# Attention and expert layer on one core: PE's turns placed between the score chunks, VectorE's remainders ahead of its maxima, row loop written out

## The reference, cut to what matters

```python
# x: (4, 2048, 256); 16 heads of 16
q, k, v = split(x @ Wqkv.T + bqkv);  q, k = rope(q), rope(k)
logits = einsum('bhid,bhjd->bhij', q, k) * SCALE
logits = einsum('bhij,gh->bgij', logits, Wpre)       # mix heads before softmax
attn = softmax(logits, axis=-1)
attn = einsum('bhij,gh->bgij', attn, Wpost)          # mix heads after softmax
out = einsum('bhij,bhjd->bhid', attn, v) -> (b, n, 256) @ Wout.T + bout
x = layernorm(x + out)
x = layernorm(x + soft_moe(x))                       # 16 experts, 16 slots
```

## Time and profile before

| | us |
|---|---|
| median of 3 runs | 9109.38 (9107.03 to 9111.76) |
| the profiled execution | 9096.98 |
| its span | 9094.8 |
| PE busy | 8336.7 (92%) |
| DVE busy | 7663.0 (84%) |
| ACT busy | 7243.9 (80%) |
| POOL busy | 5479.1 (60%) |

### The profile page before, as it was taken

The page is one execution under the profiler, slowest core; times in us unless marked ns, Lnnn a source line. Parts: engine busy times, 40 slices in busy tenths (PEclk is TensorE's granted clock), DMA queues, the critical chain, the costliest instruction groups (busy, mean ns, idle before and its releaser), DMA issues.

```text
span 9094.8 us, 401014 instructions
## 1 busy us (share of the span) xinstructions
PE 8336.7 (92%) x158060; PEld 4668.9 (51%) x158060; DVE 7663.0 (84%) x12269; ACT 7243.9 (80%) x13696; POOL 5479.1 (60%) x12005
## 2 busy tenths in 40 slices
PE   7999999997799999999779999999978999999997
PEld 4555555554455555555445555555544555555554
DVE  7888888886788888888678888888867888888886
ACT  5888888885588888888558888888856888888884
POOL 5666666663566666666356666666635666666663
PEclk9999999998899999999889999999988999999998
DMA  0000000002000000000200000000020000000002
GB/s 30 7 8 9 8 8 8 9 8 69 21 7 9 8 9 7 8 9 8 68 21 7 9 8 9 7 8 8 9 67 21 8 8 8 9 7 9 8 9 76
DMA packets 101046, 144.01 MB, mean 16 GB/s; under 512 B 8097, under 2 KB 90657, under 8 KB 96801
## 3 DMA queue, kind: packets, MB, share of 16 engines
q1 hardware_dynamic: 99104, 117.57, 3.9%
HBM read 75.60 MB, written 41.94 MB: 13 GB/s over the span
## 4 chain that ended last, share of the span: by engine, by line
PE 50%; DVE 23%; issue 15%; ACT 5%; POOL 3%; SPq 1%; DVEq 1%; DMA 1%; POOLq 1%; ACTq 0%
PE psS L1179 29%; PE psP L1199 11%; DVE top L821 7%; PE psO L1214 6%; DVE pl L861 5%; DVE big L835 5%; ACT big L648 3%; PE psM L1225 1%; ACT ph L658 1%; PE psS L1154 1%; PE psS L1311 1%; PE psS L1340 1%; ACT pr L630 1%; DVE rr L853 1%; PE psM L1239 1%
## 5 line engine op out<-in xcount | busy, mean ns | idle before, releaser
L835 DVE SCALAR_TENSOR_TENSOR big<-psP,big 128x512 f16<-128x512 f32 x4096 | 2628.1, 683 | 623.1 <-ACT big L648 610.6
L648 ACT ACTIVATE big<-psP 128x512 f16<-128x512 f32 x4096 | 2214.0, 592 | 1020.7 <-PE psO L1214 563.6
L821 DVE TENSOR_REDUCE top<-psS 128x1 f32<-128x1024 f32 x2048 | 2486.5, 1214 | 409.5 <-PE psS L1179 394.0
L1179 PE MATMUL psS<-KH,AH 128*128 128x512 f16 x8192 | 2471.9, 383 | 121.6 <-POOL AL L441 81.8
L1179 PE MATMUL psS<-KH,AL 128*128 128x512 f16 x8192 | 2448.5, 381 | 0.1
L1179 PE MATMUL psS<-KL,AH 128*128 128x512 f16 x8192 | 2446.3, 380 | 0.0
L630 ACT ACTIVATE pr<-psS,nb 128x1024 f32<-128x1024 f32 x2048 | 2281.7, 1114 | 67.9
L658 ACT ACTIVATE ph<-pr 128x1024 f16<-128x1024 f32 x2048 | 2151.2, 1050 | 32.4
L1199 PEld LDWEIGHTS psP<-rh,ph 64*128 64x128 f16 x32768 | 1434.7, 95 | 1093.1 <-issue 611.9
L861 DVE TENSOR_TENSOR pl<-pr,ph 128x1024 f16<-128x1024 f32 (+1 forms) x2048 | 1969.7, 962 | 0.6 <-ACT ph L658 0.4
L1199 PE MATMUL psP<-rh,ph 64*128 64x64 f16 x32768 | 1680.3, 192 | 213.4 <-POOL rl L535 175.0
(11 more groups left out here) (138 smaller groups left out, 7398.1 us busy)
## 6 DMA issues: line engine op xcount, KB each, us to landing
ph<-in_xT SPq DMA_DIRECT2D x16, 512.0 KB, 4.3
xr<-in_x SPq DMA_DIRECT2D x64, 128.0 KB, 2.4
d_x<-x SPq DMA_DIRECT2D x64, 128.0 KB, 1.7
d_xn<-xn SPq DMA_DIRECT2D x64, 128.0 KB, 1.7
d_lg<-lg SPq DMA_DIRECT2D x64, 128.0 KB, 1.7
d_ct<-cT SPq DMA_DIRECT2D x64, 128.0 KB, 1.7
Q<-in_w SPq DMA_DIRECT2D x8, 1024.0 KB, 12.4
out<-V SPq DMA_DIRECT2D x16, 512.0 KB, 3.3
```

The source lines that it names most:

```text
L648: a.activation(PT[:, hf * JH:(hf + 1) * JH, :, 0, i0:i0 + HQ], psP[:, ih, :].rearrange("p (j g i) -> p j g i", j=JH, g=H), ACT.Copy, scale ...
L821: v.tensor_reduce(top[:, t % 2, h:h + 1], psS[:, 2 * h:2 * h + 2, :].rearrange("p c n -> p (c n)"), X, ALU.max).then_inc(s_mx, 1)
L835: v.scalar_tensor_tensor(out=PT[:, js, :, 1, i0:i0 + HQ], in0=psP[:, ih, :].rearrange("p (j g i) -> p j g i", j=JH, g=H), scalar=MDROP, in ...
L1179: mm = pe.matmul(psS[:, c, :], A_[:, k8, k, :], K_[:, k, c * CW:(c + 1) * CW], start=n == 0, stop=n == 5)
```

## The change

PE places each turn between the two score chunks of a half (scores 0, turn 0, scores 1, scores 2, turn 1, scores 3). The four output pieces go to four places: piece 0 to the end of the slot before (t % 8 == 1), piece 1 behind scores 0, piece 2 behind scores 1, piece 3 behind scores 2 of t % 8 == 2. DVE runs the two `mixed_low` ahead of each `half_max`, `recip` behind `half_max` 0, and `low` 1 behind that. ACT runs `highs` of half 1 a slot later, between `mixed_high` 0, 1 and `bound` 0, and `highs` of half 0 behind `mixed_high` 2, 3. POOL runs `first_half`, `post` ahead of the tile preparation's high and low parts and its own `low` last. Row steps of PE, ACT and DVE move a slot earlier in several cases. The loop over the row groups is replaced by the groups written out.

```diff
-PE_SLOT = dict(y=3, turn_u=12, logits=13, turn_c=15)
-ACT_SLOT = dict(turn_u=12, weigh=14, turn_c=15)
+PE_SLOT = dict(y=3, turn_u=11, logits=12, turn_c=15)
+ACT_SLOT = dict(turn_u=11, weigh=13, turn_c=15)
 DVE_SLOT = dict(residual=4, stats=4, seed1=5, centre=6, norm1=8, norm2=8, squares=8, seed2=9,
-                keep=13, weigh=14, combine=15)
+                keep=12, weigh=13, combine=14)
...
# POOL
                     roots(t, work, 0)
                     if one:
-                        low(T - 1, t_1, first and t < 3)
+                        first_half(T - 1, t_1)
+                        post(T - 1, t_1)
                     if live:
                         mixq_high(it, t + LEAD)
+                    if one:
+                        post_high(T - 1, t_1, first and t < 5)
+                    if live:
+                        mixq_low(it, t + LEAD)
+                    if one:
+                        post_low(T - 1, t_1)
                     roots(t, work, 1)
                     if one:
-                        first_half(T - 1, t_1)
-                    if live:
-                        mixq_low(it, t + LEAD)
+                        low(T - 1, t_1, first and t < 3)
...
# ACT
                     mixed(0)
                     mixed(1)
+                    if not (first and t < 1) and (live or t < 1):
+                        highs(T - 1, (t - 1) % TI, 1, first and t < 3)
                     if live:
                         bound(T, t, 0)
                         exps(T, t, 0, early)
-                        highs(T, t, 0, early)
                     mixed(2)
                     mixed(3)
                     if live:
+                        highs(T, t, 0, early)
                         bound(T, t, 1)
                         exps(T, t, 1, early)
                         factor(T, t, early)
-                        highs(T, t, 1, early)
...
# DVE
+                    if two:
+                        mixed_low(T - 2, t_2, 0)
+                        mixed_low(T - 2, t_2, 1)
                     if live:
                         half_max(T, t, 0)
+                    if one:
+                        recip(T - 1, t_1)
                     rows(t, work, 0)
...
-                    if two:
-                        mixed_low(T - 2, t_2, 0)
-                        mixed_low(T - 2, t_2, 1)
-                    rows(t, work, 1)
                     if one:
                         low(T - 1, t_1, 1, first and t < 3)
-                        recip(T - 1, t_1)
+                    rows(t, work, 1)
+                    if two:
+                        mixed_low(T - 2, t_2, 2)
+                        mixed_low(T - 2, t_2, 3)
+                    rows(t, work, 2)
                     if live:
                         half_max(T, t, 1)
                         row_bound(T, t)
-                    rows(t, work, 2)
-                    if two:
-                        mixed_low(T - 2, t_2, 2)
-                        mixed_low(T - 2, t_2, 3)
-                    if live:
                         low(T, t, 0, first and t < 2)
...
# PE
                     if live:
                         scores(T, t, 0, first and t < 1)
-                        scores(T, t, 1, first and t < 1)
+                    piece(1)
                     if two:
                         turn(T - 2, t_2, 0, fresh)
-                    pieces(0, 1)
+                    if live:
+                        scores(T, t, 1, first and t < 1)
+                    piece(2)
...
                     if live:
                         scores(T, t, 2, first and t < 1)
-                    pieces(2)
-                    if live:
-                        scores(T, t, 3, first and t < 1)
+                    piece(3)
...
                     if two:
                         turn(T - 2, t_2, 1, False)
-                    pieces(3)
+                    if live:
+                        scores(T, t, 3, first and t < 1)
+                    piece(0)
...
# all four engines
-                with v.Fori(0, (NIT - 1) // ROWS) as turns:
-                    for k in range(ROWS):
-                        for t in range(TI):
-                            slot(turns * ROWS + (k + 1), t, False, turns * ROWS + k)
+                for it in range(1, NIT):
+                    for t in range(TI):
+                        slot(it, t, False, it - 1)
```

More of the change, by code:

```diff
@@ L43 @@
 NIT = N // (TI * QI)
-ROWS = 5
 TG = 8
@@ L548, in slot @@
                     if one:
-                        low(T - 1, t_1, first and t < 3)
+                        first_half(T - 1, t_1)
+                        post(T - 1, t_1)
                     if live:
                         mixq_high(it, t + LEAD)
+                    if one:
[4 more added lines that the diff above has]
+                        post_low(T - 1, t_1)
                     roots(t, work, 1)
                     if one:
-                        first_half(T - 1, t_1)
-                    if live:
-                        mixq_low(it, t + LEAD)
+                        low(T - 1, t_1, first and t < 3)
                     roots(t, work, 2)
-                    if one:
-                        post(T - 1, t_1)
                     if work is not None and t == POOL_SLOT["bias"]:
                         add_bias(work)
-                    if one:
-                        post_high(T - 1, t_1, first and t < 5)
                     roots(t, work, 3)
-                    if one:
-                        post_low(T - 1, t_1)
                 for t in range(LEAD):
@@ L573, in _ @@
                     slot(0, t, True, None)
-                with g.Fori(0, (NIT - 1) // ROWS - 1) as turns:
-                    for k in range(ROWS):
-                        for t in range(TI):
-                            slot(turns * ROWS + (k + 1), t, False, turns * ROWS + k)
-                for it in range(NIT - ROWS, NIT - 1):
+                for it in range(1, NIT - 1):
                     for t in range(TI):
@@ L1253, in slot, with piece @@
                     fresh = first and t == 2
-                    def pieces(*which):
-                        if t % TG == 2 and not (first and t < TG):
-                            output(T - 2, (b * NIT + it) * 2 + t // TG - 1, which)
+                    def piece(c):
+                        if t % TG == (1 if c == 0 else 2) and not (first and t < TG):
+                            output(T - t % TG, (b * NIT + it) * 2 + t // TG - 1, (c,))
                     if live:
                         scores(T, t, 0, first and t < 1)
-                        scores(T, t, 1, first and t < 1)
+                    piece(1)
                     if two:
                         turn(T - 2, t_2, 0, fresh)
-                    pieces(0, 1)
+                    if live:
+                        scores(T, t, 1, first and t < 1)
+                    piece(2)
                     if work is not None and t == PE_SLOT["turn_u"]:
@@ L1291, in _ @@
                 Tl = (b * NIT + NIT) * TI
-                output(Tl, (b + 1) * (NIT * 2) - 1, range(NC))
+                output(Tl, (b + 1) * (NIT * 2) - 1, range(1, NC))
                 for work in (y, turn_u, logits, turn_c):
```

## The result

The changed kernel takes 10621.17 us in the median (10614.34 to 10622.66, 4 runs), the kernel before 9110.57 beside it: ratio 1.1657, 95% interval 1.1642 to 1.1671. The forecast was 10460 with a range of 10290 to 10700. The profiled execution took 10622.66.

What follows compares the result with a forecast made beforehand. PE bounded the kernel before; then the ACT and DVE round trip would, at 9.22 us per tile. Row groups of 151.5 instead of 130.98 add 1348, draining 8, to 9096.98: 10453, median 10460 us, range 10290 to 10700.

Steps and rivals of the forecast that it cites:

- The round trip: ACT's mixed_high pair (H), DVE's remainders and maximum, ACT's bound and exps: 4.43 plus 4.79, 9.22 us per tile.
- PE, turns between the chunks: On PE: load stays 7.00 us per tile, every step has slack, four stands of about 0.5 us.
- Row steps: Nine DVE and ACT row steps in the cycle cost 2.6 us per row group, bounds 0 and 4.
- rival 3: POOL's rl or output pieces push turn 0 past its slack, or row steps cost double: 10700 to 10800, chance 0.12.
- Output pieces: Four pieces on PE make turn 1 late, 0.7 us twice per row group: 1.4, bounds 0 and 4.
- The first group of a batch: No row steps, one output, two slots without mixed_high and mixed_low pairs: 143.8 us.
- No loop: PE's stands of 4.02 us and half-pace chunks at eight loop jumps go, simply absent from the sum.
- PE as the bound (8700): PE stays the bound and its gaps close, so the kernel gets faster: 8700 us, chance 0.05.
- a rule of the Trainium skill's page "Perfetto Trace Analysis": Close the gaps of the busiest engine, PE; by that rule alone the time would fall.
- The falling clock: PE, less busy, drops to half pace; with a quarter of the tiles so, 11460 us; chance 0.05.
- The 76% that the prediction set against 95% for PE: PE's busy share in the new order against before, given as ground for the falling clock.

Runs made afterwards that it cites:

- Number 1: The kernel before with only DVE's slot order changed (remainders ahead of each maximum, reciprocal behind the first); ACT's order kept: 12649 us.
- Number 6: The changed kernel with PE's turns behind both score chunks of a half again, output pieces still spread: 10810.56 us, ratio 1.1872 to the kernel before.
- Number 5: The changed kernel with DVE's six row steps between remainders and second maximum moved behind low of half 0: 10373.85 us, ratio 1.14 to the kernel before.
- number 4: The changed kernel with POOL's low put back ahead of first_half and post: 10457.63 us, ratio 1.1483 to the kernel before.
- numbers 7 to 9: The kernel before with the row loop written out, 9071.86 us; then also the change's row-step slots, 8965.66; then also output pieces at four places, 8909.41.
- 2: The changed kernel with ACT's and DVE's slot orders put back to those of before, everything else as changed: 11873 us.

## Right and wrong, by the prediction's steps

- *The round trip*: right. 4.42 us for half 0 as forecast (4.43), 3.26 for H to bound 1 (3.27). ACT's waits for the maxima 2661 us (near 2600 forecast), PE 82% busy (near 80). DVE's waits for H are 1.08 us in the mean (2219.5 in 2048), just under the 1.1 to 1.4 forecast. Number 1 confirms the sum in an order that was never profiled before, within 1 us of 12650. ACT's move of `highs` without DVE's swap was not run.
- *PE, turns between the chunks*: right that they aren't in the cycle and leave short stands, of which the waits list 2.8 per tile (1348 and 1544 in 1024 tiles) where four were forecast. Number 6 shows that without them it would be 190 us slower, which the prediction didn't see.
- *Row steps*: the wrongly sized term. Forecast 2.6 us per group. Number 5 measures 247 us for six of them, 4.1 in each of 60 groups, of which 2.7 are DVE waiting for POOL's `low` (number 4). ScalarE's three (0.27, 0.48 and 0.27 us more between the maxima around slots 11, 13 and 15, means over these groups) make 1.0 more. The prediction looked only at whether `rl` comes in time when POOL's `low` moves to the end of its slot, not at which DVE instruction would then meet it. So row steps cost 5.1 instead of 2.6 us: 2.5 us x 60 = 150 of the 168 us by which the sum missed the profiled execution. To this extent rival 3 (row steps that cost double) came true beside the round trip.
- *Output pieces*: right. Forecast 1.4 us per group; over the trace's groups the second maximum of slots 2 and 10 comes 0.55 and 0.61 us late, and the first one behind slots 1 and 9 another 0.14 and 0.06, together 1.4.
- *The first group of a batch*: forecast 143.8, measured 149.9, 24 us over four batches. I counted the first two slots at 7 us each; in the first group of the four batches they take 5.6 and 15.1 in the mean. POOL still builds the leading tiles there, as it does before the change, and DVE stands 4.75 to 6.07 us for POOL's `total` in slot 1.
- *No loop*: right that its gain doesn't appear in the new time; by itself it is 32 us.
- *Rivals*: PE as the bound (8700) is refuted by the waits. The prediction put against itself a rule of the Trainium skill's page "Perfetto Trace Analysis", to find the engine with the highest occupancy and close its gaps. The section that it names, Identifying the Most-Contended Engine, has the first half of the rule; the gaps stand in the next section, Optimization Strategy. That first section also says that the busy share of the matmuls is no good measure of how near TensorE is to its peak, which the prediction leaves out. Read alone, the rule would have missed this result. It does hold where the round trips have slack: numbers 7 to 9 closed PE's gaps and gained 2.2% together. The falling clock did not come in the changed kernel (1.00 in the group's window), but it did in numbers 1, 2 and 6 (0.913, 0.948 and 0.959 in the mean), which have longer stands of PE. The 76% that the prediction set against 95% for PE left out the output pieces and row steps, which the 95% has; the group's window gives 129.49 of 154.00 us, 84%.

The sum closes: 15 groups of 153.9 instead of 151.5 and a first one of 149.9 instead of 143.8 give 4 x (36 + 6.1) = 168 us more than 10453, 10621. The group's 2.4 are the 2.5 of the row steps, with two small differences against each other: 0.3 less in the 16 tiles (9.20 us instead of 9.22) and 0.2 that no part explains. From the forecast median of 10460 the miss is 161.

## To carry to other kernels

Before two steps are swapped in a queue, write down for each pair of engines the cycle from one's result through the other's queue and back, with the handover times that the trace shows after idle times; the kernel's period is the longest of these cycles, however busy the engines are. A result that the partner waits for should be followed in the queue by enough own work that doesn't need the partner's answer: here 4.2 us of it covered 4.0, and 1.9 did not cover 3.1. And where an instruction of GpSimd is moved, look at which VectorE instruction will stand beside it.

## What the runs showed of the hardware

- VectorE and GpSimd hold each other up for whole instructions: a shift on two numbers took 0.97 us for 0.16 and `row_bound` 0.64 for 0.16, each ending with GpSimd's instruction; a subtraction that began 0.15 us behind GpSimd's took 2.08 for 1.22. The other way round, GpSimd's root step on 128x2 took 1.20 for 0.19 beside VectorE's subtraction. Maxima and remainders with an input in PSUM kept their time.
- The handover times are steady: 0.62 to 0.63 from the start of an evacuation pair to its partner, in the kernel before and in the changed one, and 1.25 to 1.26 from the start of the maximum of half 0 to `bound` 0.
- In the changed kernel PE's stands for ACT were 0.6 us in the mean and 1.7 at most, and the granted clock was 1.00 from 300 to 2500 us of the trace. With the scores together (number 6) they were 1.2 in the mean and 2.2 at most, and it was 0.97 over the same window, with stretches at the lower of the two clock levels.
